# A recommendation tower on one core: TensorE signals its summing products once per portion, and the gathers of the next tile wait for other signals

## The reference

```python
e = jnp.stack([tbl_0[ids[:, 0]], ..., tbl_31[ids[:, 31]]], axis=1)      # 1024 x 32 x 64
p = emb_inputs[:, ROW_IDX]
q = emb_inputs[:, COL_IDX]
z = jnp.einsum('bne,hne,bnh->bn', p, kernel, q)                         # 1024 x 496
h = jnp.concatenate([z, dense_ctx], axis=1)                             # 512 wide
h = jnp.maximum(h @ W_top1 + b_top1, 0.0)
h = jnp.maximum(h @ W_top2 + b_top2, 0.0)
y = h @ W_top3
```

## Time and profile before

| | |
|---|---|
| median of 3 runs | 469.64 us (468.99 to 469.8) |
| the profiled execution | 470.17 us, of which its span is 468.4 us |
| granted TensorE clock over the span | 0.967 |
| PE busy | 412.4 us (88%) |
| DVE busy | 353.3 us (75%) |
| ACT busy | 337.2 us (72%) |
| POOL busy | 242.3 us (52%) |

### The profile page before, as it was taken

The page is one execution under the profiler, slowest core; times in us unless marked ns, Lnnn a source line. Parts: engine busy times, 40 slices in busy tenths (PEclk is TensorE's granted clock), DMA queues, the critical chain, the costliest instruction groups (busy, mean ns, idle before and its releaser), DMA issues.

```text
span 468.4 us, 13663 instructions
## 1 busy us (share of the span) xinstructions
PE 412.4 (88%) x4890; PEld 307.4 (66%) x4890; DVE 353.3 (75%) x449; ACT 337.2 (72%) x2889; POOL 242.3 (52%) x260
## 2 busy tenths in 40 slices
PE   6655779788989998999989998999989998999997
PEld 6544565667757775767757765767757775667775
DVE  0236767577887978887887978887887978889982
ACT  1125856549887797949797788949797797949992
POOL 5555554555655555565555555565555555552000
PEclk9779879799999999999999999999999999999999
DMA  3456550001111011111111010111111010010000
GB/s 73 152 194 198 187 165 21 18 18 23 24 22 23 20 25 21 24 21 22 21 22 22 20 25 18 23 23 23 23 22 23 20 24 22 22 21 13 2 4 0
DMA packets 14563, 19.27 MB, mean 41 GB/s; under 512 B 7192, under 2 KB 7840, under 8 KB 14496
## 3 DMA queue, kind: packets, MB, share of 16 engines
q0 software_dynamic: 8192, 8.40, 8.3%
q1 hardware_dynamic: 6304, 10.00, 6.6%
HBM read 18.39 MB, written 0.00 MB: 39 GB/s over the span
## 4 chain that ended last, share of the span: by engine, by line
PE 54%; DVE 27%; issue 10%; another core or an unknown queue 5%; DMA 2%; POOL 1%; ACT 0%; DVEq 0%
PE u_ps L633 23%; PE u_ps L626 16%; DVE prod_t L525 12%; DVE prod_s L542 11%; PE side_ps L647 7%; DVE h L556 4%; PE side_ps L682 2%; PE u_ps L609 2%; POOL emb L388 1%; DMA emb<-tbl,ids_sb 1%; PE acc_ps L682 1%; PE side_ps L706 1%; PE u_ps L713 1%; DVE emb_t L514 0%
## 5 line engine op out<-in xcount | busy, mean ns | idle before, releaser
L437 ACT ACTIVATE prod_s<-prod_s 128x64 f32<-128x64 f32 x1405 | 310.9, 297 | 86.6 <-DVE prod_s L542 65.0
L388 POOL DMA_INDIRECT emb<-tbl,ids_sb x256 | 242.1, 946 | 184.2 <-issue 44.0
L437 ACT ACTIVATION_READ_ACCUMULATOR prod_s<-prod_s 128x1 f32 x1405 | 268.8, 225 | 3.3 <-issue 3.2
L525 DVE TENSOR_TENSOR prod_t<-u_ps,emb_t 128x1024 f32<-128x1024 f32 x128 | 154.7, 1219 | 61.9 <-remote 26.0
L626 PEld LDWEIGHTS u_ps<-emb_t,k_sb 64*128 64x128 f32 x2048 | 141.4, 194 | 53.5 <-issue 25.8
L626 PE MATMUL u_ps<-emb_t,k_sb 64*128 64x128 f32 x2048 | 154.1, 286 | 23.3 <-DVE prod_t L525 9.5
L542 DVE TENSOR_TENSOR prod_s<-u_ps,emb 128x1024 f32<-128x1024 f32 (+4 forms) x224 | 150.4, 719 | 21.2 <-PE u_ps L633 11.5
L633 PE MATMUL u_ps<-k_sb,emb_t 64*128 64x512 f32 (+5 forms) x704 | 144.0, 496 | 17.3 <-DVE prod_s L542 10.3
L633 PEld LDWEIGHTS u_ps<-k_sb,emb_t 64*128 64x128 f32 x704 | 62.0, 194 | 48.6 <-DVE prod_s L542 18.5
L647 PE MATMUL side_ps<-prod_t,pick_sb 128*32 128x256 f32 x1024 | 64.2, 382 | 0.2 <-issue 0.2
L682 PE MATMUL acc_ps<-h_t,w_sb 64*128 64x128 f32 x336 | 47.4, 278 | 0.5
(11 more groups left out here) (32 smaller groups left out, 50.9 us busy)
## 6 DMA issues: line engine op xcount, KB each, us to landing
k_sb<-k_pairs SPq DMA_DIRECT2D x9, 512.0 KB, 3.8
emb<-tbl,ids_sb POOLq DMA_INDIRECT x256
k_sb<-k_pairs SPq DMA_DIRECT2D x6, 480.0 KB, 4.4
w_sb<-w SPq DMA_DIRECT2D x1, 1024.0 KB
w_sb<-w SPq DMA_DIRECT2D x1, 512.0 KB
k_sb<-k_pairs SPq DMA_DIRECT2D x1, 448.0 KB
h<-dense SPq DMA_DIRECT2D x8, 8.0 KB
out<-y_row SPq DMA_DIRECT2D x8, 0.5 KB
```

What stands on the lines that cost most here:

```text
L388: nc.gpsimd.indirect_dma_start(emb[t % EMBS][:, f * EMBED:(f + 1) * EMBED], None, tables[f], bass.IndirectOffsetOnAxis(ap=ids_sb[:, t, f:f ...
L437: done = nc.scalar.activation(slot, slot, ACT.Copy, accum_out=to[:, column:column + 1])
L525: done = nc.vector.tensor_tensor(prod_t[at % TRING][:].rearrange("p (h x) -> p h x", h=HALVES), u, low.unsqueeze(1).to_broadcast([P, HALVE ...
```

## The change

`picked` is signalled at the end of a portion only, 4 times a tile and not 16 times. ScalarE's two waits on it, in `copy_logit` and at the end, count portions. The gather tables are written anew: no gather waits for a single pick, two wait for a portion, and some signals let two or three gathers go.

```diff
 GATHER_AT = [
-    ("u", 9), ("u", 10), ("u", 12), ("mlp", 2), ("u", 13), ("u", 14), ("u", 15), ("u", 17), ("u", 18), ("mlp", 4),
-    ("u", 19), ("u", 21), ("u", 22), ("pick", 0), ("pick", 3), ("u", 24), ("u", 26), ("pick", 4), ("pick", 7),
-    ("u", 28), ("u", 29), ("u", 31), ("pick", 10)]
+    ("u", 9), ("u", 10), ("u", 11), ("u", 12), ("mlp", 3), ("u", 13), ("u", 15), ("u", 16), ("u", 17), ("u", 18),
+    ("mlp", 5), ("u", 20), ("u", 21), ("u", 23), ("u", 23), ("u", 23), ("u", 25), ("u", 27), ("u", 27), ("u", 28),
+    ("u", 29), ("u", 31), ("u", 31)]
 OWN_GATHER_AT = [
-    ("u", 0), ("u", 1), ("u", 3), ("pick", 15), ("u", 4), ("u", 5), ("u", 6), ("u", 8), ("mlp", 0)]
+    ("portion", 2), ("u", 0), ("u", 2), ("u", 4), ("u", 4), ("portion", 3), ("u", 5), ("u", 7), ("u", 8)]
...
 SECOND_GATHERS = [
     ("u", 12), ("u", 13), ("u", 14), ("u", 15), ("turn", 5), ("u", 16), ("u", 17), ("u", 18), ("u", 19), ("u", 20),
-    ("turn", 6), ("u", 21), ("u", 22), ("u", 24), ("u", 25), ("pick", 1), ("u", 26), ("u", 27), ("pick", 5),
+    ("turn", 6), ("u", 21), ("u", 22), ("u", 24), ("u", 25), ("u", 25), ("u", 26), ("u", 27), ("u", 27),
...
                         if kind == "u":
                             pool.wait_ge(slot_filled, used(tile, at))
-                        elif kind == "pick":
-                            of = tile - 1 if at >= 3 * PORTION else tile
-                            pool.wait_ge(picked, of * NT + at + 1)
+                        elif kind == "portion":
+
+                            pool.wait_ge(picked, (t - 1) * PORTIONS + at + 1)
...
-                    act.wait_ge(picked, (t + 1) * NT + PORTION)
+                    act.wait_ge(picked, (t + 1) * PORTIONS + 1)
...
                                 start=(b == 0), stop=(b == NT - 1))
+                if stop % PORTION == 0:
                     done.then_inc(picked, 1)
```

More of the change, by code:

```diff
@@ L266 @@
 assert all(turned(t, n) < used(t, n) for t in range(TILES) for n in range(NB))
-PORTION = NT // 4
+PORTIONS = 4
+PORTION = NT // PORTIONS
 LATE_SPREAD_AT, SUMS_AT, LATE_SUMS_AT, SPREAD_AT = 4, 23, 27, 31
@@ L374, in _ @@
                         kind, at = SECOND_GATHERS[f] if t else FIRST_GATHERS[f]
[L375 to L378, removed]
+                        pool.wait_ge(slot_emptied, SLOT_USE[kind, 0, at] + 1)
                     elif t > 0:
@@ L496, in _ @@
             nc.scalar.activation(h0_t[:, T_CHUNKS:], spread_ps, ACT.Copy).then_inc(last_copied, 1)
-            act.wait_ge(picked, TILES * NT)
+            act.wait_ge(picked, TILES * PORTIONS)
             nc.scalar.activation(h0_t[:, :T_CHUNKS], side_ps[:, :T_CHUNKS], ACT.Copy).then_inc(last_copied, 1)
```

## The result

The changed kernel takes 480.07 us (median of 6, 478.09 to 481.84), before 469.64 us (468.03 to 469.98): a ratio of 1.0227, 95% interval 1.0208 to 1.0246. It is slower by 10.4 us where 3.0 had been forecast. The profiled execution took 478.97 us, 8.8 more than that of before.

What follows compares the result with a forecast made beforehand. No single engine bounds the kernel; runs of gathers delay PE's signals. Six tiles at +0.45 us give 2.7, tile 7 +0.3, tile 0 nothing: +3.0, median 472.6 us, range 464.8 to 476.0 (slightly slower case: 470.6 to 476.5).

Steps and rivals of the forecast that it cites:

- The mechanism: While gathers follow without a pause, PE's signals arrive late, about 1.8 us behind a pair's last start, 1.9 behind three's.
- turn 1: Behind u4: f26, f27 and f28 form a new run of three, so DVE sees this turn later, +1.2 us.
- u10: The run of three ahead of it becomes at most a pair, over in time, so it begins earlier: -1.1 us.
- u13: f2, f3 and f4 form a run, so its signal is seen at 329.3 against 328.88: +0.4 us.
- u20: The wait at u16 goes and only a pair stands ahead, so it starts earlier: -0.9 us.
- u24: The dearest place: f13, f14, f15 all wait for u23, so DVE gets its signal at 347.2, +1.3 us.
- next u0: Start of the following tile: comes at 359.4, +0.35 us, or +1.0 if gathers behind u31 hold it.
- The hold of u0: f21, f22 and f23 behind u31 may delay the next tile's start by some 0.7 us.
- u24 to the next u0: Tile's last stretch: 13.16 us today, 12.1 to 12.2 once the waits at u26 and u29 go.
- C: Rival, faster: u24's signal slips through between gathers and keeps u20's lead; 463.6 to 466.6, up to 468.7; chance 0.36.
- The bound of 0.7 us a tile for the signals: Upper bound on what 12 pick signals cost PE, each holding it as long as one matmul; nothing was taken.
- D: Gathers that land late: dismissed as no case of its own, f15 landing 1.4 us ahead of today; no chance given.

Runs made afterwards that it cites:

- no_gathers: The kernel before without the gathers of tiles 2 to 7, their part of the computation left out: 419.96 us, ratio 0.8947.
- run_lengths: The kernel before without the gathers of tiles 2 to 7, but with unread runs of 1 to 8 gathers behind u23 in tiles 1 to 6: 438.57 us.
- pool_plain: The kernel before with each gather of tiles 2 to 7 replaced by a plain GpSimd load of 128 rows: 420.23 us.
- u23_split: The changed kernel, but f13, f14, f15 wait for u23, portion 0 and u24, not all for u23: 470.52 us, ratio 1.0040.
- only_u23: New signalling and old tables with single picks replaced, but f13, f14, f15 all wait for u23: 482.20 us, ratio 1.0260.
- signals_16: The kernel before, its gathers' waits on single picks replaced by u23, u27 or portions, with all 16 pick signals kept: ratio 0.9937.
- pause_lengths: The kernel before without the gathers of tiles 2 to 7, but three unread gathers behind u23 in tiles 1 to 6, memset pauses between: 425.27 us.

## Why the prediction was right and wrong

**The mechanism** was right in the main: gathers that follow each other hold TensorE's signals back. `no_gathers`, `run_lengths` and `pool_plain` show it as cause and not only as a pattern in a trace. Two things it had wrong: long runs also stop TensorE's matmuls, and single gathers hold signals as well, where the prediction found no such pause.

**The places.** On the clock of the earlier trace rows (minus 6.36 us), against the kernel before, tile 5 has:

| | forecast | measured |
|---|---|---|
| turn 1 | +1.2 | +0.2 |
| u10 | -1.1 | -1.2 |
| u13 | +0.4 | -1.1 |
| u20 | -0.9 | -1.5 |
| u24 | +1.3 | +0.9 |
| next u0 | +0.35 (+1.0 with its hold) | +1.1 |

The dearest place was named: u24, and `u23_split` takes back 8.8 us there. Its time was met in part by luck. The run had four gathers and not three, its last started 0.8 us earlier than forecast, and u24 came 2.28 us behind it and not 1.9. At u13 the run of f2 to f4 did not form and no wait arose; at u18 one of 1.48 us did, behind the run f6 to f8, that I had not looked for.

**The tile's start** was met. The hold of u0, priced at 0.7, is 0.53 to 1.05 us behind tiles 1 to 6, 0.7 in the mean. The wait of 1.73 before u2 is gone and takes it in, and turn 1 comes 0.2 us later where 1.2 was forecast. So the loss does not come from there.

**The step that failed** is "u24 to the next u0": 12.1 to 12.2 us, 12.9 with the hold of u0. It took 14.60, 14.69, 12.87, 13.40, 13.31 and 13.39 us in tiles 1 to 6, 13.7 in the mean, where it was 13.15 to 13.46 before. u24 itself, counted from its tile's first matmul, is late by 1.2 us in the mean of the six, near the forecast. The sum gave back the waits at u26 and u29 and took TensorE to be ready behind u24. The hold was priced on VectorE alone. TensorE loses time as well, 1.71 and 1.87 us of stops inside u24 in tiles 2 and 5, and the waits come back at the next turn: turn 0 waits 0.73 to 2.12 us where 0.54 to 0.58 stood. In tile 5 u26 and u29 have no wait, as forecast, but turn 0 and the next u0 wait 0.73 + 1.05 us, more than the 0.21 + 0.56 + 0.81 of before.

**The clock** makes the difference between the two groups of tiles. Its lower level was granted for about 3 us in tiles 1 and 2 behind the stops in u24, and in tile 6 around 397 to 400, behind stops in u18. These tiles are 2.0, 2.7 and 2.0 us longer than before (54.79, 55.14, 54.45 against 52.83, 52.46, 52.41), the three at full clock 0.5, 1.2 and 0.8 (53.44, 53.95, 53.24 against 52.90, 52.78, 52.49). That is 9.1 us in all; tile 7 with the end gives 0.35 back (58.0 us against 58.35), where +0.3 had been forecast. What is left is the 8.8 us between the profiled executions. By an estimate from the three at full clock, the six would have 6 x 0.82 = 4.9 us without the lower clock, more than the 2.7 forecast and within its +0.35 to +1.0 a tile; the other 1.4 us in each of three tiles are 4.2 us that no term of the sum had. That the clock makes all of the 1.4 is argued, not tested by itself: in `only_u23` the same comparison gives 0.9. The Trainium skill (TensorE: Matmul & The Clock Gate, A second HAM failure mode: psum-queue depth-cycling) tells of a kernel in which frequent small idle gaps of TensorE bring the clock down and up again. The trace agrees in part: 0.50 stands behind stops of 0.32, 0.45 and 0.94 us in tile 2, but behind stops of 0.94 and 0.93 us in tile 5 it stays at 1.00. What decides between them is open.

**The rivals.** C did not happen: u24's signal slipped out between the gathers in no tile. In tile 3 it was due at 243.34, between the second gather and the third (243.01, 244.26), and came at 246.21. The bound of 0.7 us a tile for the signals was far off; the lower end, nothing, fits `signals_16`, though no run shows the reason given for it. D was no matter, as said: nothing reads the gathers of `run_lengths`, and they cost as much. The top of the range adds up to 469.64 + 6 x 1.0 + 0.3 + 0.3 = 476.2, not 476.5.

## What to carry to other kernels

On this chip an indirect gather issued by GpSimd is not free for the engines beside it even when its rows are needed much later: follow its start on the timeline, look whether what TensorE finished in the 2 us behind it is noticed late, and compare with the end of the matmuls themselves. Where a table of signals sets off gathers, the entry that matters is the one that joins two runs; change such entries one at a time and look at the longest run that comes out, not at how many gathers a signal lets go. A wait priced on the engine that waits is only its lower bound: ask whether the engine that signals can go on meanwhile, and what its clock does if it can't.

## What the runs showed of the hardware

In `run_lengths` VectorE sees TensorE's signal 2.1 to 2.9 us behind the start of the last gather of a run of three to eight. Behind a single gather a signal due 0.7 to 1.3 us after its start is seen at 1.4 to 1.5 (`pause_lengths`, three places); one due 0.4 us after it passes. A signal of VectorE's to TensorE passes within 0.05 us of the multiply's end, 0.83 us behind a gather's start. A plain load of 128 rows by GpSimd or SyncE, and a memset of 0.72 us on GpSimd, cost nothing (419.4 to 420.4 us against 419.96), and indirect gathers of 16 rows cost as much as those of 128. Starts 1.43 and 1.56 us apart hold u24 as long as starts 1.25 apart; what pause is enough for a run of three was not shown. All gathers together cost 8.3 of 52.5 us a tile. What inside the indirect form does it was not settled, nor why pauses did not help in the full kernel. The best ratios found are 0.9927 to 0.9939, the old table with its single picks replaced, with or without the new signalling and with or without short pauses; they do not differ beyond their intervals.
